# A four-row decoder layer on one core: the next row's first norm moved to the end of attention, its q and k projections moved ahead of the mixer transposes

## The reference

```python
def attention(x):                       # x: layernorm(row)
    q, k, v = x @ wq.T, x @ wk.T, x @ wv.T
    q = (q @ fq1_w.T + fq1_b) * (q @ fq2_w.T + fq2_b)      # per head
    k = (k @ fk1_w.T + fk1_b) * (k @ fk2_w.T + fk2_b)
    o = causal_linear_attention(q * scale, k, v)           # no softmax
    return rms_norm_per_head(o) * norm_w @ wo.T
def mixer(ctx, z):                      # z: layernorm(row)
    u = silu(conv4(ctx @ in_proj.T) + conv_b)
    dt, B, C = split(u @ x_proj)
    dt = softplus(dt @ dt_proj + dt_b)
    state = state * exp(dt * A) + dt * u * B               # 16 states per channel
    return (sum(state * C) + D * u) * silu(z)
def ffn(x):                             # bit_linear: int8 rows, ternary weights
    return bit_linear(silu(bit_linear(x, wg)) * bit_linear(x, wv), wo)
x = x + attention(layernorm(x))
x = x + mixer(ctx, layernorm(x))
x = x + ffn(layernorm(x))
```

## Time and profile before

| | |
|---|---|
| median of 3 runs | 1225.84 us (1223.56 to 1227.22) |
| profiled execution | 1224.94 us, its span 1223.1 us |
| mean granted TensorE clock | 0.820 |
| busy: PE, DVE, ACT, POOL | 891.3, 927.5, 585.9, 435.5 us |
| share of the span | 73%, 76%, 48%, 36% |

### The profile page before, as it was taken

The page is one execution under the profiler, slowest core; times in us unless marked ns, Lnnn a source line. Parts: engine busy times, 40 slices in busy tenths (PEclk is TensorE's granted clock), DMA queues, the critical chain, the costliest instruction groups (busy, mean ns, idle before and its releaser), DMA issues.

```text
span 1223.1 us, 11854 instructions
## 1 busy us (share of the span) xinstructions
PE 891.3 (73%) x3970; PEld 484.8 (40%) x3970; DVE 927.5 (76%) x1065; ACT 585.9 (48%) x887; POOL 435.5 (36%) x264
## 2 busy tenths in 40 slices
PE   4576765536338999988428999978528999976598
PEld 1234433413122346655222346555222356643233
DVE  4788989998989666777798666877798747863453
ACT  2787426344535753353435763453435744321332
POOL 0034544344345222535245332534245424540100
PEclk8688686756758999985758999995758999977599
DMA  9278778767435432537335432638335535550000
GB/s 322 91 182 247 173 190 227 175 191 201 101 89 130 100 86 67 125 78 198 74 80 129 113 86 55 136 87 192 72 80 138 122 86 112 130 112 0 1 9 27
DMA packets 57121, 147.20 MB, mean 120 GB/s; under 512 B 7939, under 2 KB 8323, under 8 KB 57061
## 3 DMA queue, kind: packets, MB, share of 16 engines
q0 software_dynamic: 18432, 67.12, 28.6%
q1 hardware_dynamic: 38628, 79.32, 20.5%
HBM read 74.96 MB, written 4.35 MB: 65 GB/s over the span
## 4 chain that ended last, share of the span: by engine, by line
PE 52%; DVE 25%; DMA 8%; ACT 8%; issue 6%; SPq 0%; POOL 0%; DVEq 0%; ACTq 0%; POOLq 0%
PE bank L579 21%; PE bank L743 8%; DMA ACC<-W 8%; DVE W L1370 6%; PE bank L759 5%; DVE W L1361 4%; PE bank L608 3%; PE bank L658 3%; PE bank L627 3%; PE bank L740 3%; PE bank L679 2%; DVE BST L1297 2%; ACT ARENA L1001 2%; DVE U L1320 2%; PE PB L705 1%
## 5 line engine op out<-in xcount | busy, mean ns | idle before, releaser
L1224 POOL TENSOR_TENSOR W<-W,CROW 128x1024 f32<-128x1024 f32 x128 | 310.1, 2423 | 481.5 <-DVE W L1370 481.5
L1370 DVE TENSOR_TENSOR_SCAN W<-DEC,W 128x1024 f32<-128x1024 f32 x122 | 305.0, 2500 | 0.2
L1232 POOL DMA_DIRECT2D ACC<-W x128 | 114.9, 898 | 181.9 <-DMA ACC<-W 157.5
L1361 DVE TENSOR_TENSOR W<-DU,PB 128x1024 f32<-128x1024 f32 x128 | 152.9, 1194 | 19.1 <-DMA ACC<-W 9.6
L942 ACT ACTIVATE DEC<-DT,ACOL 128x511 f32<-128x511 f32 x244 | 159.8, 712 | 6.0 <-DVE W L1370 5.9
L608 PE MATMUL bank<-IDF,ARENA 128*128 128x128 f32 x448 | 72.5, 315 | 96.8 <-DVE ARENA L1538 67.4
L743 PE MATMUL bank<-W,ARENA 128*128 128x512 fp8e4 x512 | 140.0, 398 | 0.0
L889 ACT ACTIVATE ARENA<-bank 128x512 f32<-128x512 f32 x64 | 37.9, 592 | 171.3 <-PE bank L627 79.1
L608 PEld LDWEIGHTS bank<-IDF,ARENA 128*128 128x128 f32 x448 | 62.6, 165 | 119.6 <-issue 109.0
L1459 DVE SCALAR_TENSOR_TENSOR ARENA<-bank,SDQ,ARENA 128x512 f32<-128x512 f32 x64 | 47.2, 745 | 70.8 <-PE bank L743 34.0
L1013 ACT ACTIVATE ARENA<-bank,SDQ 128x512 f32<-128x512 f32 x64 | 43.6, 686 | 75.9 <-PE bank L743 75.3
(11 more groups left out here) (152 smaller groups left out, 1396.5 us busy)
## 6 DMA issues: line engine op xcount, KB each, us to landing
ACC<-W POOLq DMA_DIRECT2D x128, 512.0 KB, 5.6
CROW<-c_rows SPq DMA_DIRECT2D x128, 256.0 KB, 3.5
W<-in_wffn SPq DMA_DIRECT2D x27, 512.0 KB, 7.1
X<-in_wffn SPq DMA_DIRECT2D x21, 512.0 KB, 5.7
ARENA<-in_x SPq DMA_DIRECT2D x4, 1024.0 KB, 9.1
X<-in_x SPq DMA_DIRECT2D x4, 1024.0 KB, 8.7
out_dram<-X SPq DMA_DIRECT2D x16, 256.0 KB, 2.0
X<-in_ctxT SPq DMA_DIRECT2D x4, 512.0 KB, 4.7
```

Source lines behind the costliest of these rows:

```text
L1224: pool.tensor_tensor(w, w, CROW[u % 2][:, :].unsqueeze(1).broadcast_to([P, 2, L]), ALU.mult)\
L1232: pool.dma_start(ACC[accumulator(u)][:, :, :], w, accum_op=ALU.add).then_inc(y_summed.sem, 16)
L1361: dve.tensor_tensor(W[u % 4][:, :, :], DU[:, 2 * h:2 * h + 2, :], PB[u % 3][:, :].unsqueeze(1).broadcast_to([P, 2, L]), ALU.mult)\
L1370: dve.tensor_tensor_scan(w, flat(decay_of(u)), w, 0.0, ALU.mult, ALU.add).then_inc(scan_done.sem, 1)
```

## The change

The first norm of row b + 1 moves. Its x rows are loaded into `X2` instead of `XB` (row 0 keeps `XB`), at SP's point j = 24 of row b behind the stores of the row before, or for row 1 at j = 29 behind `tern_done` 24. DVE takes their statistics behind the last masked scores of row b's attention, ACT makes `rstd(b + 1, 0)` behind the last `square`, and so ahead of `rms(b, 3)`. In `step`, `normed(b, 0)` is DVE's first instruction, ahead of unit r0 and `head_norm`. PE's xnT transposes go ahead of the output projection, and ACT drains them behind `step_size` 3. The q and k projections of group 0 go between units r2, r3 and r4, ahead of the yT transposes; they have banks 2 and 3, yT has 0, 1 and 4. ACT drains them behind `rstd(f, 2)` into rows 2 and 3 of `X1`. `BCR` and `BC2` move to rows 0 and 1, and in row 0 `split(0)` goes ahead of `normed(0, 0)`. The residual x rows of row 3 are loaded at j = 24 instead of j = 10.

```diff
@@ all_products
-            out += on(four, [(b, "dt", 2), (b, "dt", 3)])
+            out += on(four, [(b, "dt", 2), (b, "dt", 3)] + [(b, "xnT", k) for k in range(KT)])
         out += on(every, [(f, "wo", t) for t in range(TT)])
         if b < BATCH:
-            out += on(every, [(b, "xnT", k) for k in range(KT)])
-        out += on(every, [(f, "yT", t) for t in range(TT)])
+            out += on((2,), [(b, "q", 0)]) + on((3,), [(b, "k", 0)])
+        out += on((0, 1, 4) if b < BATCH else every, [(f, "yT", t) for t in range(TT)])
         out += on(every, ffn_products(f, b if b < BATCH else None))
-        if b < BATCH:
-            out += on(every, [(b, "q", 0), (b, "k", 0)])
@@ tiles
-        BCR = X1[0:32, 2, :]
-        BC2 = X1[0:32, 3, 0:L // 2].bitcast(bf16)
+        BCR = X1[0:32, 0, :]
+        BC2 = X1[0:32, 1, 0:L // 2].bitcast(bf16)
+        QTS, KTS = [X1[:, 2, :]] + [QT] * (GROUPS - 1), [X1[:, 3, :]] + [KTT] * (GROUPS - 1)
-        XB = part(2560, 2048).rearrange("p (t d) -> p t d", t=TT)
+        XROWS = [part(2560, 2048).rearrange("p (t d) -> p t d", t=TT)] + [X2] * (BATCH - 1)
@@ SP
+            def norm_rows(b):
+                if b == 1:
+                    sp.wait_ge(tern_done, WCH)
+                else:
+                    sp.wait_ge(*out_stored.at(b - 2))
+                sp.dma_start(XROWS[b][:, :, :], x[b].rearrange("(t p) d -> p t d", p=P)).then_inc(xb_loaded.sem, 16)
...
+                if j == 29:
+                    norm_rows(1)
             residual_rows(0)
             for b in range(1, BATCH):
                 f = b - 1
-                sp.wait_ge(*R.full_at(f, "o", GROUPS - 1))
-                sp.dma_start(XB, x[b].rearrange("(t p) d -> p t d", p=P)).then_inc(xb_loaded.sem, 16)
...
-                        else:
-                            residual_rows(b)
+                    if j == 24 and b + 1 == BATCH:
+                        residual_rows(b)
...
                     if b + 1 < BATCH and j == 24:
                         store_c(b + 1)
+                        norm_rows(b + 1)
@@ PE, step
                     step_size(b, 3)
+                    for k in range(KT):
+                        normed_T(b, k)
                     units(b, "r", 0)
                 for t in range(TT):
                     project(f, t)
                 if new:
                     units(b, "r", 1)
                     units(b, "r", 2)
-                    for k in range(KT):
-                        normed_T(b, k)
+                    qk(b, "q", 0)
                     units(b, "r", 3)
+                    qk(b, "k", 0)
                     units(b, "r", 4)
...
                 units(b, "s", 0)
-                if new:
-                    qk(b, "q", 0)
-                    qk(b, "k", 0)
@@ ACT
-                if e == 1:
+                if e == 0:
                     act.wait_ge(*bc_parts.at(b))
...
             def projections(b):
+                if b:
+                    act.wait_ge(*R.drained_at(b - 1, "yT", TT - 1))
+                else:
+                    act.wait_ge(*sp_step.at(0, 6))
...
                 square(b, GROUPS - 1)
+                if b + 1 < BATCH:
+                    rstd(b + 1, 0)
...
                         step_size(b, e)
+                    normed_columns(b)
                     decays(b, "r", 1)
-                    rstd(b, 0)
...
                 rstd(f, 2)
+                if new:
+                    projections(b)
@@ DVE
                     masked(b, g, 3)
+                    if b + 1 < BATCH and g == GROUPS - 1:
+                        rows_norm(b + 1)
                     units(b, "a", g, 6)
...
-                normed(0, 0, XB, xn_ready)
                 split(0)
+                normed(0, 0, XROWS[0], xn_ready)
...
+                if new:
+                    normed(b, 0, XROWS[b], xn_ready)
                 units(b, "r", 0)
                 head_norm(f, GROUPS - 1)
                 units(b, "r", 1)
-                if new:
-                    rows_norm(b)
                 residual(f, 0)
                 residual(f, 1)
                 units(b, "r", 2)
-                if new:
-                    normed(b, 0, XB, xn_ready)
```

More of the change, by code:

```diff
@@ L495, in residual_rows @@
                 else:
-                    sp.wait_ge(*R.drained_at(b - 1, "yT", TT - 1))
+                    sp.wait_ge(*R.drained_at(b, "k2", 0))
                 sp.dma_start(X1[:, :, :], x[b].rearrange("(t p) d -> p t d", p=P)).then_inc(x_loaded.sem, 16)
+            def norm_rows(b):
[4 more added lines that the diff above has]
+                sp.dma_start(XROWS[b][:, :, :], x[b].rearrange("(t p) d -> p t d", p=P)).then_inc(xb_loaded.sem, 16)
             def result_rows(f, t):
@@ L509, in _ @@
                 sp.dma_start(dst, src).then_inc(w_in, 16)
-            sp.dma_start(XB, x[0].rearrange("(t p) d -> p t d", p=P)).then_inc(xb_loaded.sem, 16)
+            sp.dma_start(XROWS[0], x[0].rearrange("(t p) d -> p t d", p=P)).then_inc(xb_loaded.sem, 16)
             for dst, src in ((IDF[:, :], ident), (IDB[:, :], ident16), (CAUSAL[:, :], causal),
@@ L611, in normed_T @@
             def normed_T(b, k):
-                transposes((b, "xnT", k), lambda t: XB[:, t, k * P:(k + 1) * P], [xn_ready.at(b)])
+                transposes((b, "xnT", k), lambda t: XROWS[b][:, t, k * P:(k + 1) * P], [xn_ready.at(b)])
             def qk(b, name, g):
@@ L632, in feature @@
                 key = (b, ("q1", "q2", "k1", "k2")[i], g)
-                src, of = ((QT, "q"), (KTT, "k"))[i // 2]
+                src, of = ((QTS[g], "q"), (KTS[g], "k"))[i // 2]
                 product(key, over_k(R.bank(*key)[:, :], [(FM[:, i, :], src)]), [R.drained_at(b, of, g)])
@@ L1054, in projections @@
             def projections(b):
-                drain((b, "q", 0), QT, R.bank(b, "q", 0)[:, :])
-                drain((b, "k", 0), KTT, R.bank(b, "k", 0)[:, :])
+                if b:
+                    act.wait_ge(*R.drained_at(b - 1, "yT", TT - 1))
+                else:
+                    act.wait_ge(*sp_step.at(0, 6))
+                drain((b, "q", 0), QTS[0], R.bank(b, "q", 0)[:, :])
+                drain((b, "k", 0), KTS[0], R.bank(b, "k", 0)[:, :])
             def x_proj(b):
@@ L1148, in step @@
                 exp_and_log()
-                if new:
-                    normed_columns(b)
                 decays(b, "r", 3)
@@ L1187, in step @@
                 if new:
-                    projections(b)
                     exp_and_log()
@@ L1542, in add_mixer @@
                 dve.wait_ge(*R.full_at(f, "yT", t))
-                if t == 0 and f:
-                    dve.wait_ge(*out_stored.at(f - 1))
                 dve.tensor_tensor(X2[:, t, :], R.bank(f, "yT", t)[:, :], X1[:, t, :], ALU.add)\
@@ L1550, in rows_norm @@
                 for t in range(TT):
-                    sums(b, 0, XB, t)
+                    sums(b, 0, XROWS[b], t)
                 aggregate(b, 0)
```

## The result

The changed kernel takes 1215.45 us (1213.0 to 1217.38, 5 runs), the kernel before beside it 1225.32 us (1223.56 to 1227.22, 5 runs): a ratio of 0.9907, 95% interval 0.9889 to 0.9925, 9.9 us faster. The forecast was 1214.5 us. The profiled execution took 1215.45 us, its span 1213.7 us at a mean granted clock of 0.821, against 1224.94 us, 1223.1 us and 0.820 before.

The account below looks back on a forecast made before the run. PE bounds the feed-forward tail; PE, then DVE alone, bound attention's end to the mixer transposes. Terms -2.0 + 5.1 + 0.6 + 0.6 - 4.6 - 4.6 - 6.4 = -11.3 from 1225.84 give 1214.5 us, range 1207 to 1222.5.

Parts of the forecast that it names:

- The tails: End of the feed-forward part: without q and k, PE reaches the last down projection 4.6, 4.6 and 6.4 us earlier.
- Rival (d): ACT really paces the feed-forward tail, so all 15.6 us are lost and the kernel is slower: 1230.1 us; chance 0.06.
- Row 0: Start of the kernel: split no longer waits behind normed, so ACT's step sizes and all that follows come 2.0 us earlier.
- q and k in the hole: PE's 18.9 us standstill before the mixer transposes takes both projections, 3.4 to 4.8 us each, at no cost.
- Boundaries 2 and 3: Attention's end to the mixer: output projection starts 3.4 us later, runs 0.9 shorter, normed saves 1.9; net +0.6 us each.
- Boundary 1: After row 0's attention: DVE stands still 5 us for the late x load, projection starts 8.0 later; net +5.1 us.
- Rival (a): Late x rows after row 0's attention: the load takes 12.6 us, +4.4, giving 1218.9 us; chance 0.15.
- rival (b): Transposes don't warm the clock: output projections last 16.6 us in all three rows, giving 1219.8 us; chance 0.07.
- rival (c): Half of the tails' gain is given back in attention to the chain of accumulating DMAs, +7.8: 1222.3 us; chance 0.08.

Follow-up runs that it names:

- the second profile: The changed kernel profiled again, unaltered: 1213.4 us (one run).

## Why the prediction was right, and where it was not

**The tails: right, in mechanism and size.** Forecast 4.6 + 4.6 + 6.4 = 15.6, measured 4.4 + 4.4 + 6.2 = 15.0 in all profiles. ACT became the one waited for, for 1.66 and 0.59 us, as counted. Rival (d), a tail paced by ACT, is out.

**Row 0: right.** From the drain of `xdbl` to the first product of unit 0 it was 23.5 us in both profiles before and is 21.5 us in all three of the changed kernel: the 2.0 of the forecast. (The drain itself came at 29.9 to 31.5 us in these five executions, which is the noise in the ledger's first line.) q and k in the hole delayed no DVE operation, as said.

**Boundaries 2 and 3: size off by little.** Forecast +0.6 each, measured 0 and -0.5. The term that was mis-sized is the projection's length: I took 14.5 us between bounds of 13.7 and 16.6, it was 13.9. The price of q and k at half clock, 4.8 us each, was too low as well: 16 passes take 6.87 us at full clock, so 8 take about 6.9 at half clock, an estimate. It cost nothing, since the clock was full there (3.70 and 3.60 us).

**Boundary 1: mis-sized.** Forecast +5.1 (its own terms, 8.0 - 1.1 - 1.9, give 5.0), measured +1.8, inside the bounds of +0.5 to +10.6. The load was charged 8.2 us after the nearest single load and took 5.26, and the projection 15.5 us where it took 14.0 (14.6 in another execution). The other way, `normed` took 3.07 us here and not 1.9; with the statistics one unit later it took 1.92. That DVE would stand still for it here alone was right. Rival (a) fell with it, rival (b) by the projections' 13.9 us.

**What was missing: rival (c) came true by another mechanism.** It was priced at 7.8 us and laid to the accumulating DMAs. The ledger has +6.3 us behind the tails if the profile with q and k back in the tail is counted with those of before (feed-forward start and attention together: 0 in row 0 to 1, +2.5, +2.8, and +1.0 in the last), and that kernel's own time says 4.6 us, 14.1 less 9.5. PE's busy time for the same matmuls grew by 0, 2.7, 3.4 and 1.0 us in these stretches, so it is PE work at half clock. So the forecast of 1214.5 came so near to 1215.45 by luck, because two errors cancel: about 5 us too much for the boundaries, and 5 to 6 us of clock that had no term. The sum should have had a term with both signs for the clock behind a stretch that is taken out of a fully busy PE.

**Open.** What makes the clock stay low for longer at the end of row 3's attention when the tail is short, and why it falls in the middle of attention in some executions, was not settled. All ten profiles with short tails have either the late rise or the fall in row 2's attention, and only one of four with long tails has the latter. But the fall is not peculiar to short tails: in row 1's attention all four profiles with long tails have it, the kernel before for example:

```profile
499.00:501.00 2.00, 2.00 (x4) 0.91 (x3) 1.93 (x5) 0.00 (x0) 0.85 (x1) 0.51 0.42 130
```

There the pair of rows 0 and 1 is equal (147.4 us on the mean in both kinds). So the question is rather why the kernels with long tails escape both in row 2 in three profiles of four. No run separates the length of the tail from the times at which it ends.

## What to carry to other kernels

Take work out of the stretch that PE bounds and put it into one that another engine bounds: the three tails gave 15 us (9.5 to 10 once the clock behind them is paid), and nothing else in a change of ten edits gave more than 2. Test the parts of such a change alone: the elaborate one, an earlier norm with its own load, buffer and transposes, was worth nothing beside the two projections that were moved in a few lines. Cut both profiles at the same instructions and compare several executions of each before a stretch of some 2 us is explained; where the same passes have different lengths, read the granted clock there, since a gain in one stretch can come back as a loss in the next.

## What the runs showed of the hardware

- Transposes don't keep TensorE from 2.4 GHz: with 16 of them at 1.2 GHz (3.4 us) as the last thing ahead of it, the projection's 32 passes took 13.9 us, about twice the 6.87 us of 16 at full clock. In row 1 the clock rose 8.8 to 9.6 us after the mean square began in 13 of 14 profiles, with transposes or with the projection's passes in between.
- The granted clock falls to 0.50 for about 3 us in the middle of attention with PE busy 3.00 of 3.00 us during it and 2.10 of 3.00 ahead of it (766 to 769 us of the second profile), and in other executions of the same kernel it doesn't.
- Six added matmuls raised the clock 7 us earlier (at 629 instead of 636 us) and saved nothing in three rows of four; 0.7 to 2.0 us in the fourth (30.2 us against 30.9 and 32.2), where they ran in a wait of their own.
- Two executions of one kernel can reach the same sum by different stretches: 39.5 + 108.1 and 37.0 + 110.4 us.
